# Attention scores formed once from float32 Q and K, instead of twice from stacked bf16 parts

## The chip, the cores and the metric

One core of one Trainium2 chip. The metric is the device time of one execution of the whole kernel in microseconds (us), as the median of repeated runs.

## The reference

A block of cross attention and an MLP, each added to the stream `x` of 16 samples x 128 tokens x 256 channels. Everything is float32.

```python
q, k, v = layernorm(x) @ Wq.T + bq, ctx @ Wk.T + bk, ctx @ Wv.T + bv
q, k, v = (t.reshape(B, 16, 128, 16) for t in (q, k, v))   # no transpose of heads and tokens
s = where(causal, -inf, einsum('bhqd,bhkd->bhqk', q, k) / sqrt(16))
x = x + einsum('bhqk,bhkd->bhqd', softmax(s), v).reshape(B, 128, 256) @ Wp.T + bp
h = gelu(block_quant(layernorm(x)) @ block_quant(w_fc).T + b_fc)      # 256 -> 1024
x = x + block_quant(h) @ block_quant(w_proj).T + b_proj               # 1024 -> 256
```

The reshape takes 16 heads of 128 rows x 16 channels out of a flat 128x256 buffer: row r of 8 tokens belongs to one head, and a head's 128 rows are (8 tokens) x (16 slices of 16 channels). `block_quant` rounds blocks of 32 elements to 3 bits under a shared exponent; a small error ahead of it can flip a rounding, so the attention is kept close to float32.

## The kernel before, in words

Five instruction queues (TensorE, VectorE, ScalarE, GpSimd, SP for transfers) are written out by hand, each in program order, and tied by counting semaphores. Samples go in pairs: eight pairs, one for each attention **step**. After the eight steps come 16 **tiles** of the MLP, one for each sample. A step works on pair i and, beside it, on the inputs of pair i+2 (`ahead`) and on the output projection, residual and quantisation of pair i-1.

For a pair, TensorE transposes ctx and the normalised x (`trans_c`, `trans_x`) and projects K, Q and V (`project`, L897), each into one PSUM bank as channels x tokens. ScalarE copies each out with its bias into `full` (`copy_proj`, L338). To get float32 accuracy out of bf16 matmuls, `full` is split into three bf16 parts whose sum it is: the first by VectorE (`part_a`, L649), the other two by GpSimd (`split`, L529 to L535). SP writes the nine parts to DRAM (`spill`, L245) and reads them back (`gather`, L252), which turns the layout and stacks parts of K and Q in six bands of 16 rows: a matmul over 96 rows then sums the six products of parts (`QS`, `KS`). V is stacked in three bands and folded by 32 small matmuls (`values`, L971) into `V1`, beside columns of ones that give the softmax's denominator.

A **group** k (0 to 7) of a step is four heads. `scores` puts the causal mask (L938) and four score matmuls (L941) into a bank, queries on partitions; VectorE takes the negated row maxima (`maxes`, L709). `scores_t` forms the same scores again, transposed, keys on partitions (mask L950, scores L953), and adds the maxima by a matmul of `negm` with the identity (L958). ScalarE then takes one exponential of 128x512 (`exps`, L388) into `prob`, which is already the transposed operand that `attend` (L984) needs; its four matmuls go to four column groups of the array and fill `out_b`. After each four groups ScalarE copies `out_b` to `oT` (`copy_out`, L411). Eight transfers (L303) move `oT` to `oden`, numerators and denominators by channel; ScalarE takes the reciprocal as exp(-ln) (`invert`, L394, L397), VectorE finishes it (`normalise`), TensorE projects (`project_out`), VectorE adds the residual and forms the quantised input of the MLP (`residual`, `quantise` with L758), GpSimd rounds (`round_rows`). The MLP's weights are quantised by VectorE in quarters (`round_weights`, L790) in step 0 and in the last step, and transposed by TensorE in the last (`trans_weights`).

The order of ScalarE and TensorE around the output: `attend(i, 6)` and `attend(i, 7)` close step i on TensorE, `copy_out(i, 1)` closes it on ScalarE, and `invert(i)` stands in step i+1 behind exponentials 0 and 1, two projections' copies and the copy of V.

## Time and profile before

| | us |
|---|---|
| median of three runs | 334.89 (333.96 to 336.38) |
| the profiled execution | 334.37 |
| its span, first to last instruction | 332.5 |
| TensorE busy in the span | 281.1 (85%) |
| VectorE | 217.4 (65%) |
| GpSimd | 148.6 (45%) |
| ScalarE | 137.0 (41%) |

The mean granted TensorE clock is 0.91 of full speed. All times are microseconds from the first instruction. A row of an engine's order of work gives start, duration, line, operation, what is written and read, and the number of instructions; matmuls are pipelined, so two neighbouring rows overlap, and the distance from one start to the next is what a matmul costs. A float32 matmul shows as two instructions, a transpose as one.

### The profile page before, as it was taken

The page shows a single profiled execution, that of the slowest core. Times are in us where ns is not written, and L with a number is a line of the kernel's source. Part 1 is how long each engine was busy: PE and PEld are TensorE (multiplying, and loading weights), DVE is VectorE, ACT ScalarE, POOL GpSimd, SP SyncE. Part 2 cuts the span into 40 slices and gives each one's busy share as a digit, 9 for nine tenths or more (in the row PEclk, how much of TensorE's full clock was granted, in tenths as well). Part 3 has the DMA queues.
Part 4 walks back from the last instruction along what each step waited for, and adds up shares of the span by engine and source line. Part 5 has one row for each costly group of instructions (what it writes and reads, how often), then busy time and mean ns, then how long its engine had stood idle before and what let it go on. Part 6 is the DMA issues. An engine that isn't in the chain of part 4 may idle for free.

```text
span 332.5 us, 6876 instructions
## 1 busy us (share of the span) xinstructions
PE 281.1 (85%) x2448; PEld 203.4 (61%) x2448; DVE 217.4 (65%) x419; ACT 137.0 (41%) x255; POOL 148.6 (45%) x136
## 2 busy tenths in 40 slices
PE   3828797699999999999999999795997976977744
PEld 2616585368778768768778777564672553544433
DVE  6780515943493495386476466388763999999990
ACT  2502232234344243443444432341366653666642
POOL 5042911744464462652652652032150455666664
PEclk9976989579999999999999999997796797799977
DMA  7799899998987988977996996935004000001111
GB/s 211 234 166 156 144 146 309 185 161 149 183 138 124 202 124 142 198 106 119 207 138 83 190 165 86 184 70 65 0 2 53 12 16 16 32 32 37 42 36 47
DMA packets 134936, 39.14 MB, mean 118 GB/s; under 512 B 111092, under 2 KB 134656, under 8 KB 134912
## 3 DMA queue, kind: packets, MB, share of 16 engines
q1 hardware_dynamic: 132272, 36.21, 62.5%
q10 hardware_dynamic: 2640, 2.62, 2.6%
q8 instruction: 14, 0.23, 0.3%
q14 instruction: 10, 0.08, 0.1%
HBM read 23.08 MB, written 11.53 MB: 104 GB/s over the span
## 4 chain that ended last, share of the span: by engine, by line
PE 53%; DVE 22%; issue 9%; DMA 4%; ACT 4%; SPq 4%; POOL 3%; DVEq 0%; POOLq 0%; ACTq 0%
PE bank L897 11%; PE bank L953 7%; PE bank L941 7%; PE bank L984 5%; DVE h_amax L842 4%; PE bank L950 4%; PE bank L958 4%; PE bank L997 4%; PE bank L938 4%; DVE h_exp L163 2%; PE bank L971 2%; DMA q_mem<-in_L_xattn_Wq 2%; DMA fc_rows<-in_L_ffn_w_fc 2%; DVE h_mag L166 2%; SPq L303 2%
## 5 line engine op out<-in xcount | busy, mean ns | idle before, releaser
L388 ACT ACTIVATE prob<-bank 128x512 f32<-128x512 f32 x64 | 38.3, 600 | 93.6 <-PE bank L958 88.9
L529 POOL TENSOR_TENSOR rest<-full,part 128x512 f32<-128x512 f32 x22 | 25.9, 1177 | 67.8 <-DVE part L649 67.8
L709 DVE TENSOR_REDUCE negm<-bank 128x4 bf16<-128x512 f32 x64 | 43.7, 689 | 14.0 <-PE bank L941 13.7
L578 POOL TENSOR_TENSOR k_mem<-q_mem,h_mag 128x1024 bf16<-128x1024 f32 x16 | 30.7, 1921 | 33.6 <-DVE q_mem L851 33.6
L941 PE MATMUL bank<-k_mem,q_mem 96*128 96x128 bf16 x256 | 40.7, 294 | 0.0
L953 PE MATMUL bank<-q_mem,k_mem 96*128 96x128 bf16 x256 | 40.6, 293 | 0.0
L953 PEld LDWEIGHTS bank<-q_mem,k_mem 96*128 96x128 bf16 x256 | 29.0, 117 | 9.1 <-issue 1.9
L941 PEld LDWEIGHTS bank<-k_mem,q_mem 96*128 96x128 bf16 x256 | 29.1, 118 | 8.3 <-issue 2.2
L958 PE MATMUL bank<-ident_b,negm 128*128 128x128 bf16 x256 | 27.3, 232 | 8.2 <-DVE negm L709 8.0
L897 PE MATMUL bank<-cT,wT 128*128 128x256 f32 x128 | 33.5, 407 | 0.7 <-ACT cT L354 0.7
L984 PE MATMUL bank<-prob,V 128*32 128x128 f32 x512 | 27.0, 296 | 4.2 <-ACT prob L388 2.6
L338 ACT ACTIVATE full<-bank,bias 128x256 f32<-128x256 f32 x48 | 20.2, 475 | 21.8 <-PE bank L897 21.8
L897 PEld LDWEIGHTS bank<-cT,wT 128*128 128x128 f32 x128 | 24.9, 203 | 5.4 <-issue 1.2
L958 PEld LDWEIGHTS bank<-ident_b,negm 128*128 128x128 bf16 x256 | 22.2, 109 | 9.7 <-DVE negm L709 9.6
L535 POOL TENSOR_TENSOR part<-rest,part 128x512 bf16<-128x512 f32 x22 | 25.5, 1157 | 3.1
L938 PE MATMUL bank<-mask_q,ident_b 128*128 128x512 bf16 x64 | 26.3, 411 | 0.3 <-issue 0.3
L950 PE MATMUL bank<-mask_k,ident_b 128*128 128x512 bf16 x64 | 26.4, 412 | 0.0
L531 POOL TENSOR_TENSOR part<-full,part 128x512 bf16<-128x512 f32 x22 | 26.1, 1186 | 0.0
L649 DVE CAST part<-full 128x512 bf16<-128x512 f32 x24 | 11.2, 466 | 20.9 <-ACT full L338 20.9
L842 DVE TENSOR_REDUCE h_amax<-q_mem 128x32 f32<-128x1024 f32 x16 | 19.4, 1212 | 6.9 <-ACT q_mem L454 6.9
L454 ACT ACTIVATE q_mem<-bank 128x512 f32<-128x512 f32 x32 | 18.0, 596 | 14.0 <-PE bank L1096 8.0
L1096 PE MATMUL bank<-wfcT,xqT 128*128 128x512 bf16 x64 | 22.5, 437 | 0.0
(120 smaller groups left out, 492.8 us busy)
## 6 DMA issues: line engine op xcount, KB each, us to landing
scratch<-part SPq DMA_DIRECT2D x72, 128.0 KB, 3.5
oden<-oT SPq DMA_DIRECT2D x64, 64.0 KB, 2.9
k_mem<-scratch SPq DMA_DIRECT2D x8, 384.0 KB, 4.9
q_mem<-scratch SPq DMA_DIRECT2D x8, 384.0 KB, 7.1
VS<-scratch SPq DMA_DIRECT2D x8, 384.0 KB, 9.5
k_mem<-scratch SPq DMA_DIRECT2D x8, 256.0 KB, 5.2
q_mem<-scratch SPq DMA_DIRECT2D x8, 256.0 KB, 7.5
out<-full SPq DMA_DIRECT2D x16, 128.0 KB, 1.7
```

What stands on the lines that cost most here:

```text
L388: nc.scalar.activation(prob[:, k % 2, :, :].rearrange("p g t -> p (g t)"), probT_b[k % 2][:, :], ACT.Exp, scale=SCALE).then_inc(sm["exp_do ...
L531: nc.gpsimd.tensor_tensor(part[t][1][:, :], full[t][:, :], part[t][0][:, :], ALU.subtract)\
L578: nc.gpsimd.tensor_tensor(blocks(hq[par][:, :]), blocks(hrn[par][:, :]), spread(h_mag[par][:, :], HID // BLK), ALU.subtract)\
L709: V.tensor_reduce(negm[:, k % 2, :], score_b[k % 2][:, :].rearrange("p (g t) -> p g t", g=4), axis=AX.X, op=ALU.max, negate=True).then_inc ...
L842: V.tensor_reduce(h_amax[:, :], blocks(hid[par][:, :]), axis=AX.X, op=ALU.max, apply_absolute_value=True).then_inc(sm["h_amax_done"], 1)
L897: ins = T.matmul(proj_b[t % 2][:, c * PT:(c + 1) * PT], wT[:, t, k, c, :], src[:, k, :], start=(k == 0), stop=(k == KC - 1))
L938: T.matmul(score_b[k % 2][:, :], ident_b[:, :], mask_q[:, :, :].rearrange("p g t -> p (g t)"), start=True, stop=False)
L941: ins = T.matmul(score_b[k % 2][:, g * P:(g + 1) * P], QS[par][:, head_cols(b, h)], KS[par][:, head_cols(b, h)], start=False, stop=(g == 3))
L950: T.matmul(probT_b[k % 2][:, :], ident_b[:, :], mask_k[:, :, :].rearrange("p g t -> p (g t)"), start=True, stop=False)
L953: T.matmul(probT_b[k % 2][:, g * P:(g + 1) * P], KS[par][:, head_cols(b, h)], QS[par][:, head_cols(b, h)], start=False, stop=False)
L958: ins = T.matmul(probT_b[k % 2][:, g * P:(g + 1) * P], negm[:, k % 2, g:g + 1].to_broadcast([P, P]), ident_b[:, :], start=False, stop=(g = ...
L984: ins = T.matmul(out_b[32 * g:32 * g + 32, (k % 4) * P:(k % 4 + 1) * P], V1[:, b, h, :], prob[:, k % 2, g, :], start=True, stop=True)
```

## The change

Scores are formed once, queries on partitions, straight from float32 Q and K. Heads are laid in four row groups of the array (`head_rows`): head h lies in rows 32*(h%4) to +16. `scores(i, j)` serves two groups at a time, 2j and 2j+1, whose matmuls alternate between two row groups and two banks, behind two mask matmuls; the 1/sqrt(16) is folded into Q's copy. VectorE takes maxima as before, now in float32, and ScalarE adds them as a bias for each row, in four exponentials of 128x128 for a group. The probabilities are then transposed by TensorE (`turn`) into `probT_b`, and copied to `probT` by VectorE for even groups (`copy_even`) and by ScalarE for odd ones (`copy_odd`). The splitting into parts, the second set of scores, the matmul of the maxima and `values` are gone. V is projected with tokens on partitions (`project_v`), biased by VectorE (`copy_v`), written to DRAM and read back in `V1`'s layout (`spill_v`, `gather_v`). K and Q are one float32 spill each and four gathers, one for each row group; with HL = 1 a run of a spill is 64 bytes.

The inputs are prepared one pair ahead instead of two. `attend(i, 6)`, `attend(i, 7)`, `copy_out(i, 1)` and the eight moves of `oT` now stand in step i+1, behind that step's first scores. `quantise(i)` moves to step i+2, behind its maxima 1. The MLP has buffers of its own. Of the steps only the lines after the change are shown.

```diff
-HL = 4
-NG = 2 * NH // HL
+HL = 1
+NR = 4
+NX = NH // HL // NR
+NG = 2 * NX * NR
...
+        QS = [sb(f"q_mem{n}", [P, NG // NR * P * HL]) for n in range(2)]
+        KS = [sb(f"k_mem{n}", [P, NG // NR * P * HL]) for n in range(2)]
+        V1 = [sb(f"V1_{n}", [P, 2, NH, 2 * HD]) for n in range(2)]
+        negm = sb("negm", [P, 2, 4])
+        prob = sb("prob", [P, 4, 4, P])
+        probT = sb("probT", [P, 2, 4, P])
...
+        scratch = [nc.dram_tensor(f"scratch{t}", [NG, P, RUN], f32).ap() for t in range(2)]
+        scratch_v = nc.dram_tensor("scratch_v", [2, P, E], f32).ap()
...
+            def spill(p, t):
+                sp.wait_ge(sm["proj_copied"], 2 * p + t + 1)
+                sp.dma_start(scratch[t].rearrange("g p y -> p g y"),
+                             full[t][:, :].rearrange("p (g y) -> p g y", g=NG)).then_inc(spilled[t], 16)
...
+                rows = scratch[t].rearrange("(x q) (d j) y -> q d x (j y)", q=NR, d=HD)
+                for r in range(NR):
+                    sp.dma_start(stacks[t][par][32 * r:32 * r + HD, :].rearrange("d (x z) -> d x z", z=P * HL),
+                                 rows[r]).then_inc(stacked[t], 16)
+            def spill_v(p):
+                sp.wait_ge(sm["v_copied"], p + 1)
+                for b in range(2):
+                    sp.dma_start(scratch_v[b].rearrange("(h r) e -> r h e", r=RPH), vrow[:, b, :])\
+                      .then_inc(sm["v_spilled"], 16)
+            def gather_v(p, par):
+                sp.wait_ge(sm["v_spilled"], 32 * p + 32)
+                for b in range(2):
+                    sp.dma_start(V1[par][:, b, :, 0:HD],
+                                 scratch_v[b].rearrange("(h r) (j d) -> (r j) h d", r=RPH, d=HD))\
+                      .then_inc(sm["v_stacked"], 16)
...
+            spill(0, 0)
+            gather(0, 0, 0)
+            spill(0, 1)
+            gather(0, 0, 1)
+            spill_v(0)
+            gather_v(0, 0)
+            sp.dma_start(fc_rows[:, :, :], w_fc.rearrange("(a p) e -> p a e", p=P)).then_inc(sm["fc_in"], 16)
+            def step(i, par):
+                if from_step(i, 1):
+                    move_out(i - 1)
+                if ahead(i):
+                    spill(i + 1, 0)
+                    if type(i) is not int or i < NPAIR - 2:
+                        load_ctx(i + 2, par)
+                    gather(i + 1, 1 - par, 0)
+                    spill(i + 1, 1)
+                    gather(i + 1, 1 - par, 1)
...
+                if ahead(i):
+                    spill_v(i + 1)
+                    gather_v(i + 1, 1 - par)
+            steps(sp, step)
+            move_out(NPAIR - 1)
...
+            copy_tc(0)
+            copy_w(0)
+            act.wait_ge(sm["bias_in"], 16 * 4)
+            copy_proj(0, 0)
+            copy_tx(0)
+            copy_w(1)
+            act.wait_ge(sm["bias_scaled"], 1)
+            copy_proj(0, 1)
+            copy_w(2)
...
+                act.wait_ge(sm["max_done"], GROUPS * i + k + 1)
+                if k >= 4 or from_step(i, 1):
+                    act.wait_ge(sm["t_done"], GROUPS * i + k - 3)
+                for g in range(4):
+                    ins = nc.scalar.activation(prob[:, k % 4, g, :], score_b[k % 2][:, g * P:(g + 1) * P],
+                                               ACT.Exp, bias=negm[:, k % 2, g:g + 1])
+                ins.then_inc(sm["exp_done"], 1)
+            def copy_odd(i, j):
+                act.wait_ge(sm["t_done"], GROUPS * i + 2 * j + 2)
+                nc.scalar.copy(probT[:, 1, :, :].rearrange("p g t -> p (g t)"), probT_b[1][:, :])\
+                    .then_inc(sm["odd_copied"], 1)
...
+            def step(i, par):
+                if ahead(i):
+                    copy_tc(i + 1)
+                if from_step(i, 1):
+                    copy_out(i - 1, 1)
                 exps(i, 0)
                 exps(i, 1)
                 if ahead(i):
+                    copy_proj(i + 1, 0)
+                copy_odd(i, 0)
+                if ahead(i):
+                    copy_tx(i + 1)
+                if from_step(i, 1):
                     invert(i - 1)
                 exps(i, 2)
                 exps(i, 3)
+                if ahead(i):
+                    copy_proj(i + 1, 1)
+                if is_last(i):
+                    copy_weights(0)
+                copy_odd(i, 1)
                 exps(i, 4)
+                exps(i, 5)
                 copy_out(i, 0)
+                if is_last(i):
                     copy_weights(1)
+                copy_odd(i, 2)
+                if is_last(i):
+                    copy_weights(2)
                 exps(i, 6)
                 exps(i, 7)
+                if is_last(i):
                     copy_weights(3)
+                copy_odd(i, 3)
...
+            def copy_v(p):
+                dve.wait_ge(sm["proj_done"], 3 * p + 3)
...
+                V.tensor_tensor(vrow[:, :, :], proj_b[0][:, :].rearrange("p (b e) -> p b e", b=2),
+                                bias_v[:, :].unsqueeze(1).to_broadcast([P, 2, E]), ALU.add)\
+                    .then_inc(sm["v_copied"], 1)
...
+            def copy_even(i, j):
+                dve.wait_ge(sm["t_done"], GROUPS * i + 2 * j + 1)
+                V.tensor_copy(probT[:, 0, :, :].rearrange("p g t -> p (g t)"), probT_b[0][:, :])\
+                    .then_inc(sm["even_copied"], 1)
...
+            def step(i, par):
+                zero = type(i) is int and i == 0
+                if ahead(i):
+                    stats1(i + 1)
+                if is_last(i):
+                    round_weights(1, 2)
                 maxes(i, 0)
                 maxes(i, 1)
                 if ahead(i):
+                    norm1(i + 1)
+                if from_step(i, 2):
+                    quantise(i - 2)
+                if zero:
+                    permute_wp()
+                    bias_parts(0)
+                copy_even(i, 0)
+                if is_last(i):
+                    round_weights(1, 3)
                 maxes(i, 2)
+                maxes(i, 3)
+                if zero:
+                    bias_parts(1)
+                copy_even(i, 1)
+                if zero:
+                    copy_wp()
+                    bias_parts(2)
+                    round_weights(0, 0)
+                if from_step(i, 1):
+                    normalise(i - 1)
+                maxes(i, 4)
+                maxes(i, 5)
+                if zero:
+                    round_weights(0, 1)
+                copy_even(i, 2)
+                if ahead(i):
+                    copy_v(i + 1)
+                if zero:
+                    round_weights(0, 2)
+                if type(i) is int and i == 1:
+                    round_weights(1, 0)
+                if type(i) is int and i == 1:
                     round_weights(1, 1)
+                maxes(i, 6)
+                maxes(i, 7)
+                copy_even(i, 3)
+                if zero:
                     round_weights(0, 3)
+                if from_step(i, 1):
                     residual(i - 1)
 
             steps(dve, step)
+            quantise(NPAIR - 2)
...
+            def project_v(p):
+                pe.wait_ge(sm["proj_copied"], 2 * p + 1)
+                for b in range(2):
+                    for k in range(KC):
+                        ins = T.matmul(proj_b[0][:, b * E:(b + 1) * E], cT[:, k, b * P:(b + 1) * P],
+                                       wT[:, 2, k, :, :].rearrange("p a m -> p (a m)"),
+                                       start=(k == 0), stop=(k == KC - 1))
+                ins.then_inc(sm["proj_done"], 1)
...
+            trans_w(0)
+            trans_x(0)
+            pe.wait_ge(sm["wT_out"], 1)
+            project(0, 0)
+            trans_w(1)
+            pe.wait_ge(sm["wT_out"], 2)
+            project(0, 1)
+            trans_w(2)
+            pe.wait_ge(sm["wT_out"], 3)
+            project_v(0)
...
+            def scores(i, j, par):
+                if j or from_step(i, 1):
+                    pe.wait_ge(sm["exp_done"], GROUPS * i + 2 * j)
+                for n in range(2):
+                    T.matmul(score_b[n][:, :], ident_b[:, :], mask[:, :].unsqueeze(1).to_broadcast([P, 4, P]),
+                             start=True, stop=False)
+                for g in range(4):
+                    for n in range(2):
+                        b, hs = heads(2 * j + n)
+                        rows, cols = head_rows(b, hs[g])
+                        ins = T.matmul(score_b[n][:, g * P:(g + 1) * P].rearrange("p (r j) -> p j r", r=RPH),
+                                       QS[par][rows, cols], KS[par][rows, cols], start=False, stop=(g == 3))
+                        if g == 3:
+                            ins.then_inc(sm["s_done"], 1)
+            def turn(i, k):
+                pe.wait_ge(sm["exp_done"], GROUPS * i + k + 1)
+                if k >= 2 or from_step(i, 1):
+                    pe.wait_ge(sm[("even_copied", "odd_copied")[k % 2]], 4 * i + k // 2)
+                for g in range(4):
+                    ins = T.transpose(probT_b[k % 2][:, g * P:(g + 1) * P], prob[:, k % 4, g, :], ident_f[:, :])
+                ins.then_inc(sm["t_done"], 1)
+            def attend(i, k, par):
+                pe.wait_ge(sm[("even_copied", "odd_copied")[k % 2]], 4 * i + k // 2 + 1)
+                if k == 0:
+                    pe.wait_ge(sm["v_stacked"], 32 * i + 32)
...
+            def step(i, par):
+                pe.wait_ge(sm["q_stacked"], 64 * (i + 1))
+                pe.wait_ge(sm["k_stacked"], 64 * (i + 1))
                 scores(i, 0, par)
+                if ahead(i):
+                    trans_c(i + 1, 1 - par)
+                if from_step(i, 1):
+                    attend(i - 1, 6, 1 - par)
+                    attend(i - 1, 7, 1 - par)
+                if ahead(i):
+                    project(i + 1, 0)
+                    trans_x(i + 1)
+                turn(i, 0)
+                turn(i, 1)
                 scores(i, 1, par)
...
+                attend(i, 0, par)
+                attend(i, 1, par)
+                if ahead(i):
+                    project(i + 1, 1)
+                if type(i) is int and i == 0:
+                    trans_wp()
+                if is_last(i):
+                    trans_weights(0)
+                turn(i, 2)
+                turn(i, 3)
                 scores(i, 2, par)
+                attend(i, 2, par)
+                attend(i, 3, par)
+                if ahead(i):
+                    project_v(i + 1)
+                if is_last(i):
+                    trans_weights(1)
+                turn(i, 4)
+                turn(i, 5)
+                if is_last(i):
+                    trans_weights(2)
                 scores(i, 3, par)
+                attend(i, 4, par)
+                attend(i, 5, par)
+                if from_step(i, 1):
                     project_out(i - 1)
+                turn(i, 6)
+                if is_last(i):
                     trans_weights(3)
+                turn(i, 7)
```

## Rows read from the trace of the kernel before

**Rows 1.** Stretches: busy us (count) of PE, PEld, DVE, ACT, POOL; clock; DMA share; GB/s.

```profile
34.30:70.10 35.80, 28.65 (x242) 19.61 (x241) 18.28 (x37) 9.95 (x20) 18.50 (x16) 0.78 1.03 199
...
148.70:174.80 26.10, 25.77 (x255) 19.97 (x252) 16.09 (x37) 10.74 (x21) 12.79 (x12) 1.00 0.95 151
...
252.80:332.50 79.70, 59.13 (x405) 35.65 (x402) 66.19 (x80) 43.07 (x79) 43.50 (x34) 0.84 0.13 33
220.00:240.00 20.00, 15.60 (x173) 10.92 (x174) 17.04 (x29) 5.80 (x10) 4.65 (x2) 0.83 0.21 27
```

**Rows 2.** TensorE in order of time: start, duration (us), line, operands.

```profile
34.34 0.38 PE L938 MATMUL bank<-mask_q,ident_b 128*128 128x512 bf16 x1
...
148.74 0.39 PE L938 MATMUL bank<-mask_q,ident_b 128*128 128x512 bf16 x1
148.97 0.63 PE L941 MATMUL bank<-k_mem,q_mem 96*128 96x128 bf16 x4
149.42 0.40 PE L938 MATMUL bank<-mask_q,ident_b 128*128 128x512 bf16 x1
...
150.11 0.40 PE L950 MATMUL bank<-mask_k,ident_b 128*128 128x512 bf16 x1
...
151.04 0.38 PE L938 MATMUL bank<-mask_q,ident_b 128*128 128x512 bf16 x1
...
151.72 0.62 PE L884 MATMUL bank<-perm_f,cbuf 128*128 128x128 f32 x4
152.17 0.38 PE L950 MATMUL bank<-mask_k,ident_b 128*128 128x512 bf16 x1
...
153.75 1.91 PE L897 MATMUL bank<-cT,wT 128*128 128x256 f32 x8
155.50 0.60 PE L874 MATMUL bank<-perm_f,xn 128*128 128x128 f32 x4
...
157.63 1.23 PE L971 MATMUL bank<-fold_v,VS 48*128 48x16 bf16 x32
...
160.71 0.64 PE L984 MATMUL bank<-prob,V 128*32 128x128 f32 x16
161.29 0.39 PE L950 MATMUL bank<-mask_k,ident_b 128*128 128x512 bf16 x1
```

**Rows 3.** Groups of instructions by line: count, busy us, mean ns.

```profile
L709 DVE TENSOR_REDUCE negm<-bank 128x4 bf16<-128x512 f32 x64 | 43.7, 689 | 14.0 <-PE bank L941 13.7
...
L758 DVE TENSOR_SCALAR xn<-X,mv,rs 128x256 f32 x8 | 7.7, 1004 | 0.0
...
L790 DVE TENSOR_TENSOR fc_rows<-fc_rows,w_mag 128x512 f32<-128x512 f32 x4 | 4.5, 1130 | 0.1
```

**Rows 4.** ScalarE in order of time, in a steady step.

```profile
168.71 0.60 ACT L388 ACTIVATE prob<-bank 128x512 f32<-128x512 f32 x1 [5.62 <-PE bank L958]
169.20 0.58 ACT L411 COPY oT<-bank 128x512 f32<-128x512 f32 x1
169.66 0.86 ACT L338 ACTIVATE full<-bank,bias 128x256 f32<-128x256 f32 x2
170.39 0.62 ACT L388 ACTIVATE prob<-bank 128x512 f32<-128x512 f32 x1
```

**Rows 5.** The chain of waits from 200 us: start, duration, what.

```profile
200.89 0.59 ACT oT L411
...
201.50 0.57 SPq L303
...
206.87 2.92 DMA oden<-oT
...
209.81 0.64 ACT lden L394
```

**Rows 6.** DMA from 169 to 172 us, spills alone: the packets moved.

```profile
DMA packets 4185, 0.53 MB, mean 176 GB/s; under 512 B 4185, under 2 KB 4185, under 8 KB 4185
```

**Rows 7.** The chain of waits at the end of the attention steps.

```profile
248.87 0.24 PE bank L958 x4
```

More of the change, by code:

```diff
@@ L139, in build_program @@
         h_mag = [sb(f"h_mag{n}", [P, HID // BLK]) for n in range(2)]
[L140 to L141 removed]
+        res = [sb(f"res{n}", [P, E]) for n in range(2)]
         bank = [es.enter_context(nc.psum_tensor(f"bank{n}", [P, 512], f32)) for n in range(8)]
@@ L283, in _, with move_out @@
-            sp.dma_start(pj_rows[:, :, :], w_proj.rearrange("(a p) e -> p a e", p=P)).then_inc(sm["pj_in"], 16)
-            def step(i, par, first, last):
-                if not last:
-                    if not first:
-                        sp.wait_ge(sm["st_done"], GROUPS * i)
-                    for t in range(3):
-                        gather(i + 1, 1 - par, t)
-                if ahead(i):
-                    for t in range(3):
-                        for m in range(3):
-                            spill(i + 2, par, t, m)
-                if type(i) is not int or i < NPAIR - 4:
-                    load_ctx(i + 4, par)
+            def move_out(i):
@@ L963, in values @@
-            def values(i, par):
-                pe.wait_ge(sm["v_stacked"], 16 * i + 16)
-                if ahead(i):
-                    pe.wait_ge(sm["tx_copied"], i + 3)
-                for b in range(2):
-                    for h in range(NH):
-                        n = b * NH + h
-                        ins = T.matmul(misc_b[:, n * HD:(n + 1) * HD], VS[par][:, head_cols(b, h)], fold_v[:, :],
-                                       start=True, stop=True)
-                ins.then_inc(sm["v_done"], 1)
@@ L998, in project_out, with trans_wp @@
                 ins.then_inc(sm["y_done"], 1)
-            pe.wait_ge(sm["wT_out"], 4)
-            pe.wait_ge(sm["consts"], 1)
-            def step(i, par, first, last):
-                pe.wait_ge(sm["q_stacked"], 48 * (i + 1))
-                pe.wait_ge(sm["k_stacked"], 48 * (i + 1))
-                scores(i, 0, par)
-                scores(i, 1, par)
-                scores_t(i, 0, par)
+            def trans_wp():
+                pe.wait_ge(sm["wp_permuted"], 2)
+                pe.wait_ge(sm["tx_copied"], 2)
+                for c in range(KC):
+                    for a in range(KC):
+                        ins = T.transpose(misc_b[:, (KC * c + a) * P:(KC * c + a + 1) * P],
+                                          wp_perm[:, a, c, :], ident_f[:, :])
+                ins.then_inc(sm["wT_in"], 1)
@@ L1022, in step @@
-                attend(i, 0)
-                attend(i, 1)
-                scores_t(i, 3, par)
-                scores(i, 5, par)
-                attend(i, 2)
-                if ahead(i):
-                    project(i + 2, 2)
-                if last:
-                    trans_weights(0)
-                attend(i, 3)
-                if not first:
-                    project_out(i - 1)
-                scores_t(i, 4, par)
-                scores(i, 6, par)
-                scores_t(i, 5, par)
```

496 lines of the change are left out of this document (150 added, 346 removed).

## The prediction

> **What bounds the kernel now.** I read the stretches between the starts of the steps first (which engine fills them, at what clock), then TensorE's own order of work. TensorE is the bound of the attention part: in a steady step it is busy 25.8 of 26.1 us, while VectorE has 16.1, ScalarE 10.7 and GpSimd 12.8, at the full clock of 1.00 [rows 1]. The MLP stage, the last 79.7 us, is VectorE's (66.2 us busy) [rows 1]; the diff changes its buffers and nothing of its work. So only what happens to the eight steps and to the start counts.
>
> One group of four heads costs TensorE: mask plus four score matmuls 0.68 us (148.74 to 149.42), the same for the transposed scores plus the maxima 0.92 us (150.11 to 151.04) [rows 2], together 1.6 us, eight times 12.9 us a step. Folding V costs 1.2 us more (32 matmuls from 157.63) [rows 2]. Both go. What stays: 16 passes of probabilities times V for two groups take 0.58 us, 0.29 a group; four float32 transposes 0.45 us; a float32 projection 1.75 us [rows 2].
>
> **The change on TensorE.** Added for a group: half of a pair's scores and four float32 transposes (0.45 us). A pair of groups opens with two masks (the first score matmul after a mask comes 0.23 us later [rows 2], so 0.46 us) and has eight float32 matmuls with 16 rows of contraction, a kind the trace does not have. Upper bound: a float32 matmul of 256 columns takes 1.75/4 = 0.44 us [rows 2], so 128 columns 0.22 us one behind the other. Lower bound: two row groups alternate, so at best they pair up, 0.11 us. The nearest row for matmuls that share the array is the probabilities times V: sixteen instructions in 0.58 us [rows 2], 0.036 each where one alone would be 0.11, but those load only 32 columns of weights and these 128. I take 0.18, so one pair of groups costs S = 0.46 + 8 x 0.18 = 1.9 us (bounds 1.35 and 2.25). The Trainium skill ("TensorE: Matmul & The Clock Gate", Why this matters for your kernels) says that small-K matmuls in distinct row groups run at the same time; by it S would be 1.35 and a step some 1.6 us shorter than below. The V rows agree for column groups; no row here shows row groups.
>
> TensorE's work in a step is then 4 x 1.9 (scores) + 8 x 0.45 (transposes) + 8 x 0.33 (values) + 0.9 (transposed inputs) + 3 x 1.75 + 2.0 (output projection) = 22.0 us against 25.8. If TensorE stayed the bound this would be 4 us a step won. It does not stay.
>
> **The new chain.** The next pair's scores overwrite the two banks that the exponentials read, and stand in TensorE's queue behind both turns. So one pair costs, in series: S 1.9; to VectorE 0.28; row maxima 0.65 (0.69 alone, 0.60 behind another) [rows 3]; eight activations of 128 columns; the second turn with its hand-over 0.5. The activation of 128x128 with a bias isn't in the trace. The biased one of 128x256 starts its successor after 0.37 us (169.66 to 170.39 for two) and the 128x512 after 0.49 (168.71 to 169.20) [rows 4]; halving again by that slope gives 0.30, and I bound it by 0.24 and 0.41. Eight and the tail are 2.5 us. A pair: 5.8 us; four pairs 23.3 us, still under 26.1.
>
> **The stall.** ScalarE's queue in a step is: copy of transposed ctx, copy_out(i-1, 1), exponentials 0 and 1, copy_proj, copy_odd, copy_tx, invert(i-1), exponentials 2 and on. invert waits for the eight transfers of oT, and these now start only in the same step, since copy_out(i-1, 1) waits for attend(i-1, 7), which is behind the scores of the new step. Before, the copy stood at the end of the old step and invert some 10 us later. That the eight transfers take long is in the chain of waits: the copy ends at 201.48, SP issues eight one after the other (0.67 each), the last starts at 206.87 and lands 2.92 later, invert begins at 209.81: 8.3 us [rows 5]. From the first score matmul of a step (zero): S 1.9, transposes of ctx 0.45, two attends 0.65, hand-over 0.28, copy_out 0.6: 3.9. Plus 8.3: 12.2. Invert 1.3: 13.5. Exponentials 2 and 3: 16.0. Turn 3: 16.5. Two more pairs: 28.1 us. ScalarE would have been ready for exponentials 2 at about 9, so 3 to 4 us of each step from 1 on is a wait that all engines share, with TensorE's queue blocked at turn 2, the next scores behind it. VectorE's quantise(i-2), now ahead of copy_even 0 (about 4 us: two normalisations of 1.0 [rows 3] and a chain of four smaller operations) and so of maxima 2, ends before 9.5 and is hidden by this wait; without it it would cost 0.6 us.
>
> **The clock.** In the steady step, at full clock, TensorE was 99% busy [rows 1]. It would now be 22.0/28.1 = 78%. At 78% busy (220 to 240 us) the granted clock was 0.83, in the MLP at 74% 0.84, in step 0, with its waits, 0.78 [rows 1]. On the step's chain 3S + 0.45 + 0.65 + three turns = 8.2 us are TensorE's. At a mean of 0.88, 24% of the time at 1.2 GHz, that would add 2 us; I take 1.0, since after a stall work comes in a dense row. Steady step: 29.1 us. With no fall of the clock it is 28.1. At a mean of 0.75 half of the time is at 1.2 GHz, which doubles half of the 8.2 us (+4.1) and lets TensorE's other work outgrow the waits that hide it (+0.8): 33.
>
> **Start.** The kernel before reaches its first scores at 34.3 us [rows 2] and the second step at 70.1 (where the stretches are cut [rows 1]); it projects two pairs first, and its step 0 waits for weights. After: K is projected ahead of the other weights' transposes, about 10.4 us, copied at 11.5 (its bias is in by then). Spilling it is 4,096 runs of 64 bytes. The trace has 128-byte runs at 4,185 in 3.0 us [rows 6], so 2.9 us to move and 1.4 around it, 4.3; four gathers issue in 1.8; Q's spill 4.3, with the 1.5 MB load of X beside it 6.3; gathers 1.8 more and about 1.9 to land: 28 us. Step 0 has no invert: 23.3, +3 for a half clock after the idle start, +2.7 for one weight rounding (its last operation alone takes 1.1 [rows 3]) put ahead of maxima 4 and one ahead of maxima 6, partly hidden: 29. Step 1: 29.1 + 3 for the two roundings ahead of maxima 6: 32.
>
> **SP's queue in a steady step**: eight moves end at 9.5, K spill 4.3, gathers 2, Q (copied at 16.8, after exponentials 3) spill 4.3, gathers 2, landing 1.8: 25 of 28.1 us. Hidden with 3 us to spare; V's hop comes behind it, needed only 9 us into the next step. GpSimd loses nine operations of splitting a step, VectorE loses three casts of a projection and gains four copies of a bank and one for V (0.7 each at most, as the maxima that read a bank): both off the path (VectorE is busy 16.1 of 26.1 us [rows 1]), worth nothing. In the last step the weight transposes and the last rounding add 1.4.
>
> **Sum.** 28 + 29 + 32 + 5 x 29.1 + 30.5 = 265.0. Behind the last score group the kernel before has 332.5 - 249.1 = 83.4 us [rows 7]; I keep it (the last exponential is earlier, two attends and copies are later, and quantise(6), 4 us, lies beside the first up-projections). Span 348.4, plus 1.9 around it (334.37 against 332.5): 350 us. The median before, 334.89, is 0.5 above that profiled run.
>
> **Rivals.**
> Faster (chance 0.25): row groups pair up and short activations are cheap. S = 1.4, eight activations 2.0: a pair 4.8; copy_out at 3.4, invert done at 13.0, turn 3 at 15.5, step 25.1, with the fillers (output projection 2.0) pushing 25.6; the clock stays. 28 + 28 + 29 + 128 + 27.5 + 83.4 + 1.9 = 326. It decides once the steady step is under 26.0, where the sum passes 331.5. For it: the V rows; against it: 128 columns of float32 weights for each head, and the wait of 8.3 us doesn't shrink.
> Transfers bound (0.10): if 64-byte runs to memory move at 40% of the 128-byte rate, a spill is 8.7 us and SP's chain 3.9 + 5.6 + 8.7 + 2 + 8.7 + 3.8 = 32.7 a step: +3.6 in six steps and +9 at the start, 380 us. It decides from a spill of 6.7 us. "DMA: Bandwidth & Descriptors" in the Trainium skill (Specifications) has line rate only from 512 bytes on and a read-modify-write below, which would make every short run dear. The chance is small because the 128-byte runs, under that bound too, moved at 1,400 a us [rows 6].
> Clock (0.10): TensorE falls to a mean of 0.75, a step is 33 (above), six times +3.9: 373.
> No change (0.12): in between, stall and gains of the start (some 13 us by the end of step 0) cancel at a step of 26.6: 28 + 29 + 32 + 6 x 26.6 + 1.4 + 83.4 + 1.9 = 335.
> My case (0.43): the invert wait, 335 to 360 us.
>
> Faster by over 1% (about what a measurement can tell): 0.25; within 1%: 0.12; slower: 0.63. The range runs from under the fast case to the clock case, 323 to 373.
>
> **What would show it.** Right: in a steady step ScalarE's first activation for oden (Ln) has 3 to 4 us of idle time ended by the DMA oden<-oT, TensorE's longest idle lies ahead of turn 2, starts of steps are 28 to 30 us apart, a 128x128 activation starts its successor after 0.3 us, eight score matmuls take 1.4 us behind two masks, the granted clock is under 0.95. Wrong: no idle before Ln (the moves land in time, since pairs take longer or the issues less); score matmuls at 0.11 a head; a first score before 25 or after 32 us; steps whose start waits for q_stacked; or an MLP stage whose length differs from 83 us by over 2.

## The result, and the profile after

The changed kernel takes **351.48 us** (348.62 to 353.04, four runs) against 335.63 (333.96 to 337.39) for the kernel before in the same comparison: a ratio of 1.046, 95% interval 1.037 to 1.055. Slower, and 1.5 us from the forecast of 350. The profiled execution has a span of 351.2 us and a mean granted clock of 0.85, where the kernel before had 0.91. Here and below medians and spreads are over all runs of a kernel, ratios over those within 1.5% of its fastest.

The stretches, cut at the first mask of a step's scores (columns as in [rows 1]); the six are steps 0, 1, 3, 4, 7 and the rest, where the last cut lies at VectorE's last copy of turned probabilities (267.81):

```profile
34.20:61.50 27.30, 23.54 (x189) 17.68 (x190) 15.79 (x35) 13.98 (x42) 0.00 (x0) 0.81 0.64 144
61.50:95.70 34.20, 28.36 (x211) 20.61 (x210) 19.54 (x37) 16.41 (x46) 4.29 (x2) 0.79 0.55 83
...
123.20:154.30 31.10, 26.18 (x213) 19.06 (x211) 16.48 (x40) 16.32 (x47) 2.43 (x3) 0.84 0.54 80
154.30:181.40 27.10, 23.29 (x211) 16.89 (x212) 15.88 (x38) 16.06 (x46) 2.43 (x3) 0.94 0.59 87
...
239.10:267.80 28.70, 24.48 (x204) 17.54 (x203) 16.69 (x37) 15.97 (x43) 5.37 (x3) 0.64 0.24 29
267.80:351.20 83.40, 61.02 (x438) 36.44 (x435) 71.08 (x95) 46.69 (x84) 45.15 (x36) 0.89 0.13 32
```

A steady step has TensorE busy 23.3 us where [rows 1] had 25.8, and some of the 23.3 is work at half clock (at full clock, in the stretch of e6_all below, the same work is 22.0, as forecast), so the work on the old bound did go down. But the step takes 27.1 us and not 26.1, with TensorE idle in the middle of it, and two of the five steady steps (3, above, and 6) take about 31, at a clock of 0.84. Here is step 4 on TensorE in order of time:

```profile
154.27 0.60 PE L937 MATMUL bank<-mask,ident_b 128*128 128x512 bf16 x2
154.81 1.16 PE L943 MATMUL bank<-k_mem,q_mem 16*128 16x128 f32 x16
155.90 0.66 PE L877 MATMUL bank<-perm_f,cbuf 128*128 128x128 f32 x4
...
168.67 2.15 PE L954 MATMUL bank<-ident_f,prob 128*128 128x128 f32 x8 [3.00 <-ACT prob L386]
170.61 1.06 PE L937 MATMUL bank<-mask,ident_b 128*128 128x512 bf16 x2
...
172.69 0.65 PE L966 MATMUL bank<-probT,V 128*32 128x128 f32 x16
...
176.23 0.59 PE L937 MATMUL bank<-mask,ident_b 128*128 128x512 bf16 x2
```

Sixteen score instructions, eight heads, cover 154.81 to 155.90, behind two masks in 0.54. The step's hole lies between 165.67 and 168.67, ahead of turn 2, as forecast, and the first work behind it runs at half speed (granted clock 0.50 from 168.67 to 171.6): the two turns take 1.94 us where the forecast had 0.9, the two masks 0.99 where step 4 began with 0.54. The score matmuls that follow are back at 1.09. The hole is ScalarE's wait:

```profile
158.63 2.17 ACT L386 ACTIVATE prob<-bank,negm 128x128 f32<-128x128 f32 x8 [0.85 <-DVE negm L683]
160.64 1.22 ACT L344 ACTIVATE full<-bank,bias 128x256 f32<-128x256 f32 x2
161.57 0.70 ACT L392 COPY probT<-bank 128x512 f32<-128x512 f32 x1
162.10 0.66 ACT L355 COPY xnT<-bank 128x512 f32<-128x512 f32 x1
166.29 0.63 ACT L398 ACTIVATE lden<-oden 128x512 f32<-128x512 f32 x1 [3.53 <-DMA oden<-oT]
...
167.49 2.15 ACT L386 ACTIVATE prob<-bank,negm 128x128 f32<-128x128 f32 x8
```

Ln (L398, `lden`) stands behind copy_tx and starts at 166.29, 12.0 us into the step, after a wait of 3.53. Exponentials 2 and 3 start behind it. What it waited for is in the chain of waits of the next step, the same order as [rows 5], now inside the step:

```profile
184.37 0.54 ACT oT L415
...
184.92 0.64 SPq L287
...
190.00 3.23 DMA oden<-oT
...
193.26 0.64 ACT lden L398
```

The copy of `out_b`, eight issues on SP (the first issue and the last landing are shown), the last move's landing, Ln: 8.9 us from start to start, as in [rows 5]. Over the run ScalarE waited for these moves in all seven steps that have them (columns: total us, times, longest):

```profile
ACT lden L398 <- DMA oden<-oT: 26.7, 7, 4.8
```

And the start, from the chain of waits (start, duration): K's projection, K's spill, Q's spill, the first masks.

```profile
9.63 3.43 PE bank L892 x8
...
14.32 4.50 DMA scratch<-full
...
21.25 9.28 DMA scratch<-full
...
34.18 1.01 PE bank L937 x2
```

### The profile page after: what moved, and what is told of

It reads as the page before. It is cut to its first block, busy times and chain, and to the rows that moved or that the text cites. A ratio compares the mean times of both kernels' runs of the same rounds, so it can differ in the third digit from the quotient of the medians.

```text
span 351.2 us, 6322 instructions
## 1 busy us (share of the span) xinstructions
PE 271.9 (77%) x2128; PEld 190.6 (54%) x2128; DVE 210.9 (60%) x419; ACT 180.2 (51%) x455; POOL 72.8 (21%) x70
## 4 chain that ended last, share of the span: by engine, by line
PE 37%; DVE 20%; DMA 12%; SPq 11%; ACT 10%; issue 7%; POOL 1%; DVEq 0%; ACTq 0%; POOLq 0%
SPq L287 10%; PE bank L943 9%; PE bank L954 8%; DMA oden<-oT 7%; DVE h_amax L830 5%; ACT prob L386 5%; PE bank L937 4%; DMA scratch<-full 4%; PE bank L966 3%; DVE h_exp L156 3%; PE bank L981 3%; PE bank L901 3%; PE bank L892 3%; DVE h_mag L159 2%; DVE hrn L839 2%
## 5 line engine op out<-in xcount | busy, mean ns | idle before, releaser
L386 ACT ACTIVATE prob<-bank,negm 128x128 f32<-128x128 f32 x256 | 69.4, 382 | 44.2 <-DVE negm L683 44.2
L954 PE MATMUL bank<-ident_f,prob 128*128 128x128 f32 x256 | 46.5, 324 | 31.2 <-ACT prob L386 31.1
L688 DVE COPY probT<-bank 128x512 f32<-128x512 f32 x32 | 22.1, 690 | 75.7 <-PE bank L954 75.7
L683 DVE TENSOR_REDUCE negm<-bank 128x4 f32<-128x512 f32 x64 | 41.2, 685 | 33.2 <-PE bank L943 33.0
L954 PEld LDWEIGHTS bank<-ident_f,prob 128*128 128x128 f32 x256 | 33.9, 163 | 42.8 <-ACT prob L386 40.5
L943 PEld LDWEIGHTS bank<-k_mem,q_mem 16*128 16x128 f32 x512 | 37.3, 219 | 18.1 <-issue 18.1
L943 PE MATMUL bank<-k_mem,q_mem 16*128 16x128 f32 x512 | 44.1, 319 | 0.0
L567 POOL TENSOR_TENSOR hq<-hrn,h_mag 128x1024 bf16<-128x1024 f32 x16 | 30.7, 1919 | 27.3 <-DVE hrn L839 27.3
L937 PE MATMUL bank<-mask,ident_b 128*128 128x512 bf16 x64 | 24.1, 466 | 13.3 <-DMA q_mem<-scratch 13.2
L966 PE MATMUL bank<-probT,V 128*32 128x128 f32 x512 | 23.5, 305 | 1.1 <-ACT probT L392 0.8
L480 ACT COPY hqT<-bank 128x1024 bf16<-128x1024 bf16 x16 | 16.2, 1012 | 12.3 <-PE bank L1108 12.2
```

Source lines behind the costliest of these rows:

```text
L386: ins = nc.scalar.activation(prob[:, k % 4, g, :], score_b[k % 2][:, g * P:(g + 1) * P], ACT.Exp, bias=negm[:, k % 2, g:g + 1])
L567: nc.gpsimd.tensor_tensor(blocks(hq[par][:, :]), blocks(hrn[par][:, :]), spread(h_mag[par][:, :], HID // BLK), ALU.subtract)\
L683: V.tensor_reduce(negm[:, k % 2, :], score_b[k % 2][:, :].rearrange("p (g t) -> p g t", g=4), axis=AX.X, op=ALU.max, negate=True).then_inc ...
L937: T.matmul(score_b[n][:, :], ident_b[:, :], mask[:, :].unsqueeze(1).to_broadcast([P, 4, P]), start=True, stop=False)
L943: ins = T.matmul(score_b[n][:, g * P:(g + 1) * P].rearrange("p (r j) -> p j r", r=RPH), QS[par][rows, cols], KS[par][rows, cols], start=Fa ...
L954: ins = T.transpose(probT_b[k % 2][:, g * P:(g + 1) * P], prob[:, k % 4, g, :], ident_f[:, :])
```

## The experiments

The changed kernel was run again beside the first group: 352.12 us (350.44 to 360.33), before 336.4, ratio 1.046 (1.039 to 1.053). "Less than the changed kernel" below is against this 352.12, also where the other run was on another chip. Its five steady steps took 29.0, 30.6, 27.2, 27.3 and 30.1 us.

> The changed kernel once more, beside the experiments on the same chip, as the reference for all of them: 349 to 353 us, steps of 27 to 31 us.

**e1_invert_later.** It tests the theory of the stall against a wait that was hidden anyway.

```diff
 # ScalarE, step
-                if from_step(i, 1):
-                    invert(i - 1)
                 exps(i, 2)
...
                 copy_odd(i, 1)
+                if from_step(i, 1):
+                    invert(i - 1)
                 exps(i, 4)
 # VectorE, step: normalise(i - 1) from ahead of maxes(i, 4) to behind maxes(i, 5)
```

> Only the places of invert(i-1) (ScalarE: behind exponentials 2, 3 and copy_odd 1, ahead of exponentials 4) and of normalise(i-1) (VectorE: behind maxima 5) change. Theory of the stall: ScalarE's wait for the moves of oT (3.5 us ahead of Ln in each step) disappears, turn 2 follows project(i+1, 1) at once, and the clock stays up. By the step at 154 us of the changed kernel the chain of pairs is then 7.1 + 3 x 5.2 = 22.7 us, but SP's queue needs 25.1 us from a step's first scores until Q has landed (154.3 to 179.3), so the next scores wait for Q's stack and the steps become 25 to 26 us: 351 - 6 x 3.3 = about 331 us (328 to 336). Rival 1, the wait was hidden behind something else anyway: no change, 349 to 353. Rival 2, SP's queue is no bound: steps of 23 us, 317 us.

Measured: 339.89 us (336.40 to 342.83), ratio 1.009 (1.006 to 1.012) to the kernel before; 12.2 us less than the changed kernel, where 20 were expected. ScalarE's wait for the moves is gone from its list of waits. The direction and the next bound were right and the size wrong: the steps are 27.3 and 26.6 us in the stretch read and 26.3 to 29.0 in the other three, not 25 to 26. The chain of waits of one step, from its moves to the next step's scores:

```profile
150.43 0.62 SPq L287
...
156.53 5.69 DMA scratch<-full
...
164.11 4.64 DMA scratch<-full
...
170.06 2.28 DMA q_mem<-scratch
...
172.45 0.60 PE bank L937 x2
173.06 1.93 PE bank L943 x16
```

It is SP's queue from end to end, as expected, but 27.3 us long, not 25.1: with TensorE waiting for Q's stack at the end of a step, the next step begins at half clock (scores 1.93 us), and copy_out, on which the moves hang, starts 4.7 us into the step (149.82) instead of 2.9.

**e2_filled_wait.** The wait stays, its effect on the clock is to go. The twelve added matmuls are work that no output uses.

```diff
                 if ahead(i):
                     project(i + 1, 1)
+                if ahead(i) and from_step(i, 1):
+                    for _ in range(12):
+                        T.matmul(misc_b[:, :], ident_b[:, :], mask[:, :].unsqueeze(1).to_broadcast([P, 4, P]),
+                                 start=True, stop=True)
```

> The wait stays; twelve bf16 mask matmuls of 512 columns into misc_b, whose result nobody reads, are put behind project(i+1, 1) in steps 1 to 6, 2.6 us of work in TensorE's idle time ahead of turn 2. Theory that the half clock behind the stall is a cost of its own: Ln still starts 12 us into the step, but the granted clock of a step rises from 0.83 to 0.94 to nearly 1.00, turn 2 and the scores behind it run at 2.4 GHz (1.1 us less for two turns, 1.1 less for scores), all steps come to 26 to 27 us instead of 27 to 31: about 339 us (335 to 343). Rival, the clock is a symptom and costs nothing because the chain is ScalarE's and SP's: 349 to 353; or, if the added work outlasts the wait, slower.

Measured: 342.51 us (340.63 to 344.76), ratio 1.022 (1.014 to 1.029) to the kernel before: 72 more matmuls take 9.6 us off the changed kernel. ScalarE still waited 25.0 us for the moves in seven steps, so the wait is there; TensorE's order of work shows the filling:

```profile
158.37 1.99 PE L892 MATMUL bank<-xnT,wT 128*128 128x256 f32 x8
160.20 2.75 PE L1019 MATMUL bank<-mask,ident_b 128*128 128x512 bf16 x12
163.17 0.66 PE L954 MATMUL bank<-ident_f,prob 128*128 128x128 f32 x4 [0.22 <-ACT prob L386]
```

and four of the five steady steps are now alike, 26.1 to 26.3 us at full clock, two of them in a row here:

```profile
149.00:175.00 26.00, 24.58 (x222) 17.33 (x223) 15.79 (x38) 15.91 (x46) 2.43 (x3) 1.00 0.61 90
174.80:201.00 26.20, 24.77 (x226) 17.53 (x225) 16.22 (x39) 16.04 (x46) 2.43 (x3) 1.00 0.62 90
```

The fifth, step 3, still took 30.3 us at a clock of 0.89. The twelve matmuls did not outlast ScalarE's wait, which was 4.73 us there, and behind what was left of the hole the clock fell again:

```profile
133.90 0.65 PE L954 MATMUL bank<-ident_f,prob 128*128 128x128 f32 x4 [1.59 <-ACT prob L386]
...
135.51 1.06 PE L937 MATMUL bank<-mask,ident_b 128*128 128x512 bf16 x2
...
142.64 1.04 PE L954 MATMUL bank<-ident_f,prob 128*128 128x128 f32 x8
```

So the wait costs twice: once by its own length, and once by the half clock behind it. That second part is 1 us in the short spells (27.1 against 26.0). In the long ones (31.1) the difference is 5 us, of which 1.2 is a longer wait (4.75 us in step 3 against 3.53 in step 4) and some 4 the clock's. Over the whole, filling the hole gave back 9.6 us, beside the 16 us that the change lost.

**e3_group_by_group.** Do alternating row groups overlap?

```diff
                 for n in range(2):
                     T.matmul(score_b[n][:, :], ident_b[:, :], mask[:, :].unsqueeze(1).to_broadcast([P, 4, P]), start=True, stop=False)
-                for g in range(4):
-                    for n in range(2):
+                    for g in range(4):
                         b, hs = heads(2 * j + n)
```

> The changed kernel with the same matmuls in another order: mask and four score matmuls of the even group, then those of the odd group, so neighbours lie in one row group of the array instead of two. Changed kernel: sixteen instructions in 1.09 us. Theory, alternating row groups overlap: the eight heads now take about twice the time of a lone one, 1.7 to 1.8 us (0.22 a head), a pair's scores 2.3 us instead of 1.6. Rival, the 0.136 a head is the pace of loading 128 columns of weights and has nothing to do with row groups: the eight heads stay at 1.1 us. The time in either case changes little, since the even group's maxima can start earlier: 350 to 356 by the theory, 347 to 351 by the rival.

Measured: 391.98 us (390.74 to 398.48), ratio 1.164 (1.161 to 1.167). Of the two the theory fits, and my estimate of the time was far off. A pair at full clock, up to the masks of the next:

```profile
165.76 0.38 PE L937 MATMUL bank<-mask,ident_b 128*128 128x512 bf16 x1
166.07 1.15 PE L942 MATMUL bank<-k_mem,q_mem 16*128 16x128 f32 x8
167.15 0.39 PE L937 MATMUL bank<-mask,ident_b 128*128 128x512 bf16 x1
167.47 1.15 PE L942 MATMUL bank<-k_mem,q_mem 16*128 16x128 f32 x8
168.56 0.64 PE L965 MATMUL bank<-probT,V 128*32 128x128 f32 x16
...
171.09 1.04 PE L953 MATMUL bank<-ident_f,prob 128*128 128x128 f32 x8
171.97 0.38 PE L937 MATMUL bank<-mask,ident_b 128*128 128x512 bf16 x1
```

Four heads in one row group take 1.09 us (166.07 to 167.15 and 167.47 to 168.56), exactly what eight heads in two alternating row groups took: 0.27 against 0.136 us a head. The edit also lets neighbours write one bank instead of two, and no run separates that; the V rows, which overlap within one bank (0.036 us each [rows 2]), speak against the bank as the cause. The 0.27 is more than the 0.22 that I had as upper bound for a lone stream. The Trainium skill says ("TensorE: Matmul & The Clock Gate", Part 3) that a weight load overlaps running matmuls only where the row group differs. The 0.27 would fit that, but no run here times a load apart, so it isn't shown as the cause. Why 40 us and not 4: a pair's scores grow by 1.2 us at full clock and by about twice that at half, and 32 pairs stand in series. The even group's earlier maxima save nothing, because TensorE has no slack to take them up: in the pair above it has no idle time from 165.76 to 171.97, although the last exponential was done at 170.5. So its own order of work sets the pace there.

**e4_start.** The start alone.

```diff
 # TensorE
-            trans_x(0)
             pe.wait_ge(sm["wT_out"], 1)
             project(0, 0)
+            trans_x(0)
 # ScalarE: the load of X[4:16] from behind copy_w(2) to behind copy_w(0)
```

> Only the start changes: TensorE projects K ahead of transposing x, and the 1.5 MB load of X goes out behind the first weight copy (about 8 us) instead of beside Q's spill. In the changed kernel K was copied at 14.3 us and Q's spill took 9.3 us instead of K's 4.5. Theory, the start is on the path with its whole length: first scores at 27 to 29 us instead of 34.2, total 344 to 347. Rival, what the start wins is lost to a longer stretch at half clock in step 0: 349 to 352.

Measured: 345.99 us (342.63 to 349.72), ratio 1.024 (1.016 to 1.032) to the kernel before, 6.1 less than the changed kernel; first scores at 29.9 us instead of 34.2. K's copy starts 1.4 us earlier (11.70 against 13.14). X's load now lies beside K's spill, which takes 6.8 us, and Q's takes 4.7: together 2.2 less than before the edit. The expected 27 to 29 was too early by 1 us, and the total is in the range.

**e5_sp_order.** The next bound behind e1. SP's spill of K of the next pair is issued inside move_out.

```diff
             def move_out(i, between=None):
...
+                        if between and 2 * g + n == 5:
+                            between()
```

> e1_invert_later, and in SP's queue K's spill of the next pair goes out behind the fifth of the eight moves instead of behind the eighth. In e1_invert_later a step from its first scores (145.2) to the next (172.5) is SP's chain from end to end: moves 6.0 us, K spill 5.7, gathers 1.8, Q spill 4.6, gathers, landing 2.3; the first scores waited for q_mem in five steps (28.1 us with the start). Theory, SP's queue is the bound there: K's spill starts 1.5 to 2 us earlier and steps go from 27.2 to about 25.4 us, 328 us (325 to 333). Rival 1, the runs of spill and moves share the transfer engines, so the spill takes longer by what it starts earlier: 337 to 341. Rival 2, steps are bound by the clock that falls while TensorE waits: 335 to 340.

Measured: 332.64 us (329.77 to 333.95), ratio 0.987 (0.982 to 0.992), so 1.3% under the kernel before and 7.3 us less than e1_invert_later, in the range but at its end. Two of its steady steps took 23.9 and 24.3 us at full clock, the other three 27.2 to 27.9 at 0.87 to 0.89. SP's queue was the bound of e1's steps, and where the clock is up its release shows in full.

**e6_all**, with e4's start added.

> e5_sp_order and e4_start together: if the gains are of different stretches they add up, 328 - 6 = 322 us (319 to 328), under the kernel before. If the start only moves work into a half clock, as e5_sp_order.

Measured: 330.72 us (324.21 to 333.69), over the range of 319 to 328. Its four runs scatter over 9 us and three of them lie over 1.5% above the fastest, so no ratio is given; e6_again below settles the size. Within one execution its steps are alike in work and unlike in clock:

```profile
142.10:166.10 24.00, 22.03 (x213) 16.21 (x212) 16.91 (x40) 16.48 (x47) 2.44 (x3) 1.00 0.64 90
...
193.00:220.60 27.60, 24.99 (x213) 18.19 (x211) 16.16 (x39) 16.12 (x46) 2.43 (x3) 0.88 0.55 78
```

**e7_more_moves.** The dose: twelve moves instead of eight, the four added ones to a tile that nobody reads.

```diff
                 sp.wait_ge(sm["o_copied"], 2 * i + 2)
+                for g in range(4):
+                    sp.dma_start(odup[:, :, :, 32 * g:32 * g + 32].rearrange("p c b x -> p (c b) x"),
+                                 oT[32 * g:32 * g + HD, :, :, :, :].rearrange("p j b k r -> p (j b k r)"))\
+                      .then_inc(sm["o_moved"], 16)
 # every wait on o_moved counts 192 a step instead of 128
```

> The changed kernel with twelve moves of oT instead of eight: four copies of the same size into an unused tile stand ahead of the eight, 2.8 us of SP's queue in each of seven steps. By the theory of the stall (copy_out, moves, invert, exponentials 2 in series) every one of steps 1 to 7 grows by 2.8 us and by what the longer wait takes from the clock, ScalarE's wait ahead of Ln goes from 3.5 to 6.3 us: 351 + 7 x 2.8 = 371 us (368 to 378). Rival, the moves have slack: 350 to 354.

Measured: 380.60 us (377.32 to 385.08), ratio 1.124 (1.121 to 1.127): 28.5 us more than the changed kernel, a little over the range of 368 to 378. The wait ahead of Ln:

```profile
ACT lden L403 <- DMA oden<-oT: 48.6, 7, 7.7
```

It grew by 21.9 us (from 26.7) over seven times, 3.1 each. The remaining 7 us come with a lower clock (mean 0.82 instead of 0.86). I had put that part too low again; no run separates it here.

**e6_again, e8_q_spill_first, e9_q_first_filled**, side by side on one chip. e6_again is the kernel of e6_all, e8 adds the first edit below to it, e9 both.

```diff
 # e8, SP's step
+                    spill(i + 1, 1)
                     gather(i + 1, 1 - par, 0)
-                    spill(i + 1, 1)
                     gather(i + 1, 1 - par, 1)
 # e9, TensorE's step, besides
                     project(i + 1, 0)
+                    for _ in range(3 if from_step(i, 1) else 0):
+                        T.matmul(misc_b[:, :], ident_b[:, :], mask[:, :].unsqueeze(1).to_broadcast([P, 4, P]), start=True, stop=True)
                     trans_x(i + 1)
```

> e6_all once more beside the next two, with more rounds: 324 to 333 us, the spread from the granted clock of single steps (24.0 us a step at full clock, 27 to 28 at 0.87 to 0.89).

> e6_all with Q's spill ahead of K's gathers in SP's queue. There Q was copied at 155.1 us of the trace and its spill issued at 157.2, behind the four gathers of K. Theory, SP's chain still ends each step (the scores at 166.1 waited 0.4 us for q_mem at full clock, TensorE idle before): Q's stack lands 2 us earlier, steps of 24.0 become 23.5 and TensorE's work gets no wait at the step's end, so fewer half-clock stretches: 3 to 8 us less than e6_all, 320 to 327. Rival, TensorE's own order of work is the bound and the clock falls for waits inside the step: within 2 us of e6_all.

> e8_q_spill_first, and three bf16 mask matmuls of 512 columns into misc_b, whose result nobody reads, fill the 0.95 us in which TensorE waits for the normalised x behind project(i+1, 0). Theory, half clock costs 3 to 4 us a step in which it falls: filled, fewer steps fall, 2 to 6 us less than e8_q_spill_first. Rival, it falls for waits elsewhere (exponentials ahead of the turns): no change, or 1 us more.

Measured: 327.47 us (324.25 to 330.18), 321.02 (319.04 to 322.94) and **317.32** (313.99 to 323.84), ratios to the kernel before 0.972 (0.968 to 0.977), 0.954 (0.950 to 0.958) and 0.943 (0.939 to 0.946). e6_again had three steady steps of 23.8 to 24.6 us and one of 25.3 at full clock, and one of 27.1 at 0.87, which is the picture of e6_all once more. Q's earlier spill gave 6.5 us, the filling 3.7, both within what the theories had. For e8 the share of a shorter chain and of a fuller clock wasn't separated; for e9 the mean clock over all runs went from 0.90 only to 0.91, so that the gain came by the clock is likely and not shown. The starts of steps 2, 3 and 4 in e9, 24.5 and 25.4 us apart at full clock; step 3 still waited 0.89 us for Q's stack:

```profile
83.57 0.59 PE L940 MATMUL bank<-mask,ident_b 128*128 128x512 bf16 x2
...
108.08 0.60 PE L940 MATMUL bank<-mask,ident_b 128*128 128x512 bf16 x2 [0.89 <-DMA q_mem<-scratch]
...
133.43 0.60 PE L940 MATMUL bank<-mask,ident_b 128*128 128x512 bf16 x2
```

The change with all its repairs (and 18 matmuls that do nothing) is 19 us under the kernel before.

## Why the prediction was right, step by step

**The stall: right.** Ln at 12.0 us of step 4 (12.2 forecast), a wait of 3.53 us ahead of it (3 to 4; in steps 2, 3 and 6 it was 4.2 to 4.8), the third pair's scores at 16.3 (16.5). e1 took the wait away and gained 12 us; e7 lengthened it by 3.1 us a step and lost 28.

**Sizes inside the chain: two errors that cancel against the clock.** I took 0.18 us a head; it is 0.136, nearer the lower bound of 0.11, and by e3 alternation makes it so. A pair's masks and scores are 1.63 us, where I took 1.9. The Trainium skill ("TensorE: Matmul & The Clock Gate", Why this matters for your kernels) has small-K matmuls in distinct row groups run at the same time, which gave 1.35: the trace agrees in kind and lies between. Eight activations of 128x128 take 2.0 us (158.63 to 160.64), 0.25 each, not 0.30, so the slope from 512 to 256 columns [rows 4] doesn't continue as I drew it. A pair was thus 5.2 to 5.6 us instead of 5.8. I added it up from scores, maxima, exponentials and turn in series; but in the last pair of step 4 TensorE has no idle time from 176.23 to 181.39, so there its own order of work (scores, values, output projection, turns) sets the 5.2 us. With the wait and without the fall of the clock the step is 26.0 (e2), not 28.1.

**The clock: right in kind, too small.** I charged 1.0 us a step. The five steady steps are 27.5, 31.1, 27.1, 27.1 and 30.6, mean 28.7, against 26.0 with the hole filled: 2.7 us a step, of which some 0.4 is that ScalarE's waits were longer (4.1 us on average, against 3.7 in e2's four steps at full clock). My 29.1 came out within 0.4 of the mean because the chain was 2.1 too long while these two took 1.7 more than I charged. That is luck, and the reader should weigh it so.

**The start: wrong by 6 us.** First scores at 34.2 us, not 28, no earlier than before [rows 2] and past the 32 that I had named as a sign of being wrong. K's projection took 3.43 us (9.63 to 13.06) instead of 1.75, half the pace of a steady step though the clock records show 1.00 there, and stood behind the transposes of x; and Q's spill took 9.3 us, not 6.3, with the load of X beside it. Before, the same projection ran at full pace at that time:

```profile
10.25 1.89 PE L897 MATMUL bank<-cT,wT 128*128 128x256 f32 x8
11.97 1.89 PE L897 MATMUL bank<-xnT,wT 128*128 128x256 f32 x8
```

e4, which moved the transposes and the load together, shows 4.3 of the 6.2 us to be avoidable and on the path. The slow projection stayed (3.6 us). Step 0 was 27.3 (29) and step 1 34.2 (32).

**SP's queue: right that it was hidden, by less than I said.** K's spill lands 5.4 us after issue in step 4 and Q's 4.5 (4.3 each forecast). Without the stall, in e1, it was the bound at once. The rival of slow 64-byte runs (a spill of 8.7 us) is out: the median over the 16 spills is 5.0.

**The last step and the MLP: right as a sum.** 112.1 us from the last step's scores to the end, 113.9 forecast. The MLP stage keeps its length: from its first up-projection to the end it is 80.0 us, before 81.0. The last step itself ran at half clock from 244.9 to 263.3 us, behind a hole of 3.5, for which I had charged 1.0 us; so here too, as I read it, a chain taken too long stood against a clock taken too cheap.

**The sum: the errors cancel.** In the profiled execution the start was 6.2 us over, step 0 was 1.7 under, step 1 2.2 over, the five steady steps 2.0 under, the last step with the MLP 1.8 under: together a span of 351.2 against 348.4. The direction and the cause were foreseen; that the total came within 1.5 us was luck.

**The rival "faster"** had nearly the right sizes (0.12 a head, 2.0 us for eight activations) and missed for its other condition, that the clock stays up. With the clock held up by filling in four of five steady steps, and the wait still there, the kernel is 342.5, not 326. In e2's profiled execution (340.6) the start is 5.3 us over that rival's sum, step 1 1.8, step 3 with its half clock 4.7, and the other four steady steps some 0.5 each.

What stays open is how long the half clock lasts: some 3 us in steps 2, 4 and 5, 9 to 10 in steps 3 and 6. These steps were not equal. In 3 and 6 SP took 6.8 and 6.6 us for its eight moves (one single issue took 1.8 us in step 3), in the others 5.8 to 5.9, and TensorE's hole ahead of turn 2 was 4.2 and 4.0 us instead of 3.0 to 3.6. But the hole's length alone doesn't decide it: in e2 a hole of 1.6 us was followed by 7.4 us at half clock, and when the changed kernel was run again its step 6 took 30.1 us after a hole of 2.9. No run explains it.

## What to carry to other kernels

When work is taken off the busiest engine, look in the new order of every queue for the pair "issued late, waited for early": here a copy moved behind the next step's scores while its consumer stayed early in the queue of ScalarE, and against 3.8 us less matmul work a step stood a wait of 3.5 us and the half clock behind it. Price a hole on TensorE twice, by its length and by the half clock behind it (here 1 to 4 us), and try at once what happens when it is filled with matmuls nobody needs: that gives the price of the clock alone, as far as the filling covers the hole. Don't take a sum that comes out for a sum that is right: compare it term by term. And after each repair read the chain of waits again: ScalarE's wait gave way to SP's queue, that to the clock.

## What the runs showed of the hardware that was not expected

- Float32 matmuls with 16 rows of contraction and 128 columns: 0.136 us a head when neighbours alternate between two row groups (and two banks), 0.27 in one row group (and one bank).
- An activation with a bias by row, 128x128 out of PSUM, starts its successor after 0.25 us, where 128x256, also with a bias, took 0.37 and 128x512 without one 0.49 [rows 4].
- SP issues one of the moves of `oT` to `oden` (64 KB) each 0.62 to 0.82 us, so eight are 6 us of one queue (5.9 in step 4); the place of a spill among them is worth 7 us of the whole (e5 against e1).
- At 9.6 to 13.1 us of the changed kernel matmuls run at half pace while the records give a clock of 1.00, so the records of that stretch can't be relied on.
- A copy of a projection out of PSUM (`full`, 128x256) takes 0.72 us with HL = 1, where it lays down single elements, and took 0.475 with HL = 4, in runs of four.
